# A Mamba and feed-forward layer: the shift of both layer norms computed on POOL in two operations instead of on VectorE in two

## What is computed

```
def _layernorm(x, axis=-1, eps=1e-05):
    m = jnp.mean(x, axis=axis, keepdims=True)
    v = jnp.var(x, axis=axis, keepdims=True)
    return (x - m) / jnp.sqrt(v + eps)

h = _layernorm(x) * (1 + ca) + sa
x = x + ga * mamba(h)
h = _layernorm(x) * (1 + cb) + sb
x = x + gb * ffn(h)

# inside mamba, for every channel e, state n and row t:
s = s * dA[t, e, n] + dBu[t, e, n]
y[t, e] = sum over n of s[e, n] * C[t, n]
```

## Time and profile before

| | |
|---|---|
| median of 3 runs | 2017.89 us (2012.1 to 2021.84) |
| the profiled execution: its time | 2014.19 us |
| the profiled execution: its span | 2012.5 us |
| busy share of the span | VectorE 92%, POOL 91%, TensorE 88%, ScalarE 76% |
| mean granted TensorE clock | 0.97 of full speed |

### The profile page before, as it was taken

The page is one execution under the profiler, slowest core; times in us unless marked ns, Lnnn a source line. Parts: engine busy times, 40 slices in busy tenths (PEclk is TensorE's granted clock), DMA queues, the critical chain, the costliest instruction groups (busy, mean ns, idle before and its releaser), DMA issues. The chain is left out here.

```text
span 2012.5 us, 29641 instructions
## 1 busy us (share of the span) xinstructions
PE 1768.9 (88%) x9128; PEld 1316.4 (65%) x9128; DVE 1861.3 (92%) x2219; ACT 1537.4 (76%) x4897; POOL 1823.4 (91%) x757
## 2 busy tenths in 40 slices
PE   7986888989888898988989898898988889898798
PEld 5665757667576765757666675766757676575664
DVE  2798999999999999999999999999999999999995
ACT  3766778797877869778787877878787786977763
POOL 1789999999999999999999999999989999999993
PEclk9897999999999999999999999999999999999899
DMA  5655514032140412304042240403214041220300
GB/s 172 236 121 148 148 42 157 22 126 74 52 138 24 140 47 95 105 22 157 22 143 68 111 137 26 157 22 127 73 58 132 28 139 46 95 79 23 126 27 32
DMA packets 72003, 186.19 MB, mean 93 GB/s; under 512 B 6818, under 2 KB 8482, under 8 KB 63908
## 3 DMA queue, kind: packets, MB, share of 16 engines
q1 hardware_dynamic: 68148, 176.95, 25.8%
q0 software_dynamic: 3696, 7.34, 2.2%
HBM read 172.20 MB, written 12.06 MB: 92 GB/s over the span
## 5 line engine op out<-in xcount | busy, mean ns | idle before, releaser
L596 POOL TENSOR_TENSOR ub<-u,b_all 128x2048 f32<-128x2048 f32 x255 | 1167.8, 4579 | 47.1 <-DMA b_all<-bc_scratch 47.1
L752 ACT ACTIVATE decay<-dt,decay_rate 128x256 f32<-128x256 f32 (+1 forms) x2048 | 880.7, 465 | 6.0 <-DVE state_p L1503 5.4
L1503 DVE TENSOR_TENSOR_SCAN decay<-decay,carry,ub 128x512 f32<-128x512 f32 x589 | 735.5, 1275 | 11.5 <-ACT decay L752 10.5
L614 POOL TENSOR_TENSOR state_p<-state_p,c_all 128x1024 f32<-128x1024 f32 (+1 forms) x256 | 529.8, 2070 | 103.3 <-ACT carry L736 79.0
L1503 DVE TENSOR_TENSOR_SCAN state_p<-decay,carry,ub 128x512 f32<-128x512 f32 x435 | 538.3, 1269 | 38.9 <-ACT decay L752 38.4
L1070 PE MATMUL y_bank<-ident,sc_d 128*128 128x128 f32 x2356 | 351.6, 282 | 94.3 <-DVE sc_d L1518 94.3
L1518 DVE TENSOR_TENSOR sc_d<-decay,c_all 128x512 f32<-128x512 f32 x589 | 378.1, 677 | 13.1 <-PE y_bank L1070 4.4
L1070 PEld LDWEIGHTS y_bank<-ident,sc_d 128*128 128x128 f32 x2356 | 279.4, 145 | 143.3 <-DVE sc_d L1518 131.7
L1070 PE MATMUL y_bank<-ident,state_p 128*128 128x128 f32 x1740 | 247.1, 283 | 106.9 <-POOL state_p L614 105.3
L1070 PEld LDWEIGHTS y_bank<-ident,state_p 128*128 128x128 f32 x1740 | 204.2, 145 | 203.6 <-POOL state_p L614 148.0
L736 ACT ACTIVATE carry<-decay 128x2 f32<-128x2 f32 x589 | 96.4, 164 | 313.3 <-DVE sc_d L1518 313.3
(11 more groups left out here) (141 smaller groups left out, 1837.9 us busy)
## 6 DMA issues: line engine op xcount, KB each, us to landing
win_h<-win_m SPq DMA_DIRECT2D x128, 256.0 KB, 2.6
win_z<-win_m SPq DMA_DIRECT2D x128, 256.0 KB, 2.9
b_all<-bc_scratch SPq DMA_DIRECT2D x31, 1024.0 KB, 4.7
c_all<-bc_scratch SPq DMA_DIRECT2D x31, 1024.0 KB, 5.4
xa<-x SPq DMA_DIRECT2D x16, 512.0 KB, 5.1
xc<-x SPq DMA_DIRECT2D x16, 512.0 KB, 3.8
out<-xc SPq DMA_DIRECT2D x15, 512.0 KB, 3.8
ffn<-factors POOLq DMA_DIRECT2D x7, 1024.0 KB, 9.9
```

The lines of the kernel that those rows point to most:

```text
L596: pool.tensor_tensor(ub[:, slot, :, :, :], u[:, (PAIRS * c + q) % U_PAIRS, :, :].unsqueeze(1).to_broadcast([P, QUAD, 2, ROWS]), b_all[:, n ...
L614: pool.tensor_tensor(part, part, c_all[:, n:n + k, :].unsqueeze(2).to_broadcast([P, k, 2, ROWS]), ALU.mult).then_inc(pooled, 1)
L752: last = act.activation(bk[:, j * ROWS + j:(j + 1) * ROWS], dt[:, pair % DT_PAIRS, j, j:], ACT.Exp, scale=decay_rate[:, e, n:n + 1])
L1503: dve.tensor_tensor_scan(dst, bk[:, :], ub[:, quad % UB_RING, i, :, :].rearrange("p j r -> p (j r)"), carried_in[:, n, 2 * q:2 * q + 1], A ...
```

## The change

`shifts` is removed from VectorE. POOL's `deviations` gets two more operations for both halves at once: minus r (r times a constant tile of -1), and that times the mean. Each waits for the one ahead of it. The `nrm` tiles get a third row, and a norm counts 4 on its semaphore as it did before (2 + LB = 4).

```
-NORMS = 2 + LB
+NORMS = 4
...
-        nrm_a = sb("nrm_a", [P, 2, LB])
+        nrm_a = sb("nrm_a", [P, 3, LB])
...
-            for i, value in enumerate((-0.5, EPS)):
+            for i, value in enumerate((-0.5, EPS, -1.0)):
...
                 pool.wait_ge(normed, NORMS * c + 1)
                 pool.tensor_tensor(nrm[:, 0, :], nrm[:, 0, :], small[:, 0, :], ALU.pow).then_inc(normed, 1)
+                pool.wait_ge(normed, NORMS * c + 2)
+                pool.tensor_tensor(nrm[:, 2, :], nrm[:, 0, :], small[:, 2, :], ALU.mult).then_inc(normed, 1)
+                pool.wait_ge(normed, NORMS * c + 3)
+                pool.tensor_tensor(nrm[:, 1, :], nrm[:, 2, :], mv[:, :, 0], ALU.mult).then_inc(normed, 1)
...
-            def shifts(c, mv, nrm, normed):
-
-                dve.wait_ge(normed, NORMS * c + 2)
-                for t in range(LB):
-                    dve.tensor_scalar(nrm[:, 1, t:t + 1], mv[:, t, 0:1], nrm[:, 0, t:t + 1], -1.0,
-                                      ALU.mult, ALU.mult).then_inc(normed, 1)
...
-            shifts(0, mv_a, nrm_a, norm_a)
...
-                    if c == 0 and s == 2:
-                        shifts(1, mv_a, nrm_a, norm_a)
...
-                    if c + 2 < CHUNKS and s == 28:
-                        shifts(c + 2, mv_a, nrm_a, norm_a)
...
-                    if lc is not None and s == 20:
-                        shifts(c - 1, mv_c, nrm_c, norm_c)
```

More of the change, by code:

```diff
@@ L220, in build @@
         cond_h = sb("cond_h", [P, KD, BATCH])
-        small = sb("small", [P, 2, LB])
+        small = sb("small", [P, 3, LB])
         bias_row = sb("bias_row", [BATCH, DIM])
@@ L257, in build @@
         mv_c = sb("mv_c", [P, LB, 2])
-        nrm_c = sb("nrm_c", [P, 2, LB])
+        nrm_c = sb("nrm_c", [P, 3, LB])
         warm = sb("warm", [P, 1])
```

## The result

The changed kernel takes 2020.2 us (median of 20 runs, 2018.3 to 2021.69) against 2016.76 us for the one before (20 runs, 2012.1 to 2021.84). The ratio is 1.0017 with a 95% interval from 1.001 to 1.0023: 3.4 us slower, between 2.0 and 4.6 us. The forecast was 5.5 us slower, which it called "the same". A second set on another chip gave 2019.17 us (12 runs) against 2014.92 us, ratio 1.002 [1.0009, 1.0032].

What follows compares the result with a forecast made beforehand. A once-a-chunk loop was the bound: POOL's work up to the tap, then VectorE and ScalarE in turn. 7.56 + 1.08 - 3.12 = +5.5 us, 2023.4 us from a median of 2017.89 us; range 2012 to 2031 us.

Steps and rivals of the forecast that it cites:

- The price of the two operations: On POOL behind r: the two added operations cost 0.54 us a norm, bounded by 0.34 and 0.92 us.
- The path at the end of a chunk: POOL's stretch to quad 15's product, then TensorE, ScalarE, VectorE's tap: 0.54 us later, 14 times, 7.56 us.
- Where VectorE would see it: At VectorE's convolution tap, which waits for ScalarE's copy_h: the wait grows from 0.99 to about 1.5 us.
- The first norm's removed shifts: VectorE step 28: removal gains nothing; VectorE only waits 0.84 instead of 0.60 us at the scan behind.
- The second norm: VectorE step 20: 0.24 us gained in chunks 2 to 14, 3.12 us; POOL's added work at quad 9 hidden there.
- Chunks 1 and 15: Second norm there: POOL's 0.54 us is paid each time, the shift's 0.24 us not earned; 1.08 us slower.
- VectorE as the bound: Rival: every one of 31 removed shift pairs counts 0.24 us, 7.4 us less, 2010.5 us; chance 0.12.
- Both sides hidden: Rival: 0.54 us of slack on TensorE or ScalarE between 683 and 700; no change, 2017.9 us; chance 0.12.
- POOL in every chunk: Rival: second norm also costs 0.54 us in all 15 chunks, 3.1 us not earned; +15.7 us, 2033.6 us; chance 0.14.

Runs made afterwards that it cites:

- e1_first: Against the kernel before: only the first norm's shift moved to POOL, the second norm's kept on VectorE; 2026.03 us, ratio 1.0049.
- e3_added: The kernel before, all shifts kept on VectorE, plus two idle POOL multiplies behind the first norm's power; 2028.06 us, ratio 1.0057 to the kernel before.
- e2_second: Against the kernel before: only the second norm's shift moved to POOL, the first norm's kept on VectorE; 2015.65 us, ratio 0.9998.
- e4_quad9: The changed kernel plus four idle POOL multiplies at quad 9, behind the second norm; 2030.64 us, ratio 1.0069 to the kernel before.
- e5_quad13: The changed kernel plus four idle POOL multiplies at quad 13, behind the first norm; 2047.85 us, ratio 1.0151 to the kernel before.

## Why the prediction was right

**The price of the two operations: right.** 0.55 us measured, 0.54 us forecast, down to the 0.77 us of the first multiply. The forecast's gloss that the waits between the operations make the price is right in part. Dependent multiplies start 0.28 us apart, and one whose follower does not wait holds POOL 0.15 us. So two without any wait would take some 0.3 us (an estimate from these rows), and the waits are under half of the 0.55 us.

**The path at the end of a chunk: right in direction, 0.07 us too dear.** POOL's product, TensorE's projection and ScalarE's `tanh_gate` all came later, as said, in chunks 3 to 14. The step "nothing in POOL's stretch absorbs it, so TensorE, ScalarE and the tap come 0.54 us later" missed a small wait of TensorE for VectorE behind the product. 0.48 us came through, not 0.54 (`e1_first`, `e3_added`).

**Where VectorE would see it: wrong.** The tap's wait was to grow to about 1.5 us; it stayed at 0.99 us. The forecast followed the long way over ScalarE and missed the short one: TensorE, late by the same amount, empties the `sc_d` ring late, and VectorE waits 0.39 us there. The size is the same either way. The forecast's own test ("I am wrong if the tap's wait does not grow") was a bad test: the period was the right one.

**The first norm's removed shifts: right.** They are worth nothing (`e1_first` equals `e3_added` in its chunk), and the wait they went into is the one named, up from 0.60 to 0.84 us.

**The second norm: right.** 0.24 us a chunk, at quad 11, in both the changed kernel and `e2_second`; the added POOL work at quad 9 is hidden, with about 0.8 us to spare (`e4_quad9`). POOL's wait of 0.45 us at quad 10 is gone and that at quad 12 is 1.41 us. TensorE's waits for POOL there did grow (from 2.50 us at 766.23 to 2.78 us at 768.05, with a new one of 0.40 us at 773.77), but nothing came of it.

**Chunks 1 and 15: not borne out as put.** The 3.53 us for which TensorE waits at 288.05 lie in a place where the clock is at half for 6.8 us in the kernel before and for 3.4 us in the changed one, which gets 1.3 us back there, so a term of 0.54 us can't be read there. The shift's 0.24 us, said not to be earned in these two chunks, is gained at quad 11 of both. In chunk 15, `e2_second` shows its scans 2.31 us ahead of the kernel before in quads 6 to 8 and 1.78 us at the end: net 0.53 us lost, as forecast, out of 0.24 us gained and more than that lost behind it. In both profiles of the changed kernel nothing is lost from quad 10 of chunk 15 to its last scan; ahead of that lie the 1.7 us of the clock.

**The sum.** The rows show the 0.48 us 12 times and the 0.24 us in the 13 chunks of the forecast: 12 x 0.48 - 13 x 0.24 = +2.6 us. So the forecast's +5.5 us was too high by 0.06 us in each of its 14 terms (0.8 us), by the terms paid in chunks 1 and 2, for which the rows show none that can be told from the clock or none at all (1.0 us), and by the 1.08 us of chunks 1 and 15, which the changed kernel does not show. Measured were +3.4 [2.0, 4.6]; what the chunks leave over, some 0.8 us, is not assigned. That the total fits so well is partly luck. The two profiled executions differ by 5.35 us (2019.54 and 2014.19), and 3.2 us of this are the two places above at the end, where the clock fell in both profiles of the changed kernel. The kernel before has its own such losses in other executions: its median lies 2.6 us above its profiled one, that of the changed kernel 0.7 us. That these balance is argued, not shown.

**The rivals.** VectorE as the bound (-7.4 us) falls: step 28's shifts are worth nothing. Both sides hidden (0 us) falls: the chunk is 0.24 us longer. POOL in every chunk (+15.7 us) falls: the 0.24 us of the second norm are earned, and TensorE's wait at quad 10 appears only with the four more multiplies of `e4_quad9`.

**What stays open** is what decides where in a chunk the clock falls. Edits of 0.2 to 1 us a chunk moved these stretches, with 10 us and more for the total in `e5_quad13`, and no rule was found that foretells the place.

## What to carry to other kernels

On an engine that others wait for, a chain of tiny operations costs more than their number says: 0.28 us for one that waits for the one ahead of it, 0.15 us for one whose follower does not wait. Move such a chain only to a place with slack behind it. The engine's own idle time does not tell how much there is (it was 1.41 us, and cover ended after 0.8 us), so check the place by adding more (`e4_quad9` against `e5_quad13`). When a wait is shortened, look for the limit next behind it before counting the gain: here 0.92 us taken off POOL's path gave 0.1 us. And read the effect of a small change from the period of an undisturbed repetition; the totals here moved by more than the change did.

## What was not expected of the hardware

In a kernel whose TensorE is busy 88% of the time, its clock still falls to half for stretches of 3.4 us behind waits of 0.9 to 2.5 us. Whether one costs 1.7 us or nothing depends on what it lies on. The runs of the kernel before, which lie 9.5 us apart on one chip, are the slower the lower their mean granted clock is. But with the waits filled and most of the stretches between 330 and 1850 us gone, the median was no better. A 128x2 multiply on POOL lasts 0.20 us, as long as a 128x1 operation on VectorE.
